# Cross-attention of a decoder layer: row maxima turned once per unit and placed by a transfer, values and totals one group later

## The reference, cut to what matters

```python
q = (x @ Wq).reshape(B, N, HEADS, hd).transpose(0, 2, 1, 3)
k = (context @ Wk).reshape(B, M, HEADS, hd).transpose(0, 2, 1, 3)
v = (context @ Wv).reshape(B, M, HEADS, hd).transpose(0, 2, 1, 3)
scores = jnp.einsum('bhid,bhjd->bhij', q, k) * scale
scores = jnp.where(context_mask[:, None, None, :], scores, max_neg)
attn = jax.nn.softmax(scores, axis=-1)
out = jnp.einsum('bhij,bhjd->bhid', attn, v)
out = out.transpose(0, 2, 1, 3).reshape(B, N, DIM)
return out @ Wo
```

## Time and profile before

| | |
|---|---|
| median of 3 runs | 3777.01 us (3770.28 to 3780.96) |
| profiled execution | 3775.88 us, span 3774.1 us, mean granted clock 0.982 |
| TensorE busy | 3639.7 us, 96% of the span, 28244 instructions |
| VectorE, ScalarE, GpSimd | 63%, 46%, 35% |
| hardware transfer queue | 318.26 MB, 30.7% of 16 DMA engines |

### The profile page before, as it was taken

How to read it: one execution, slowest core, us unless ns; L and a number is a source line. 1 busy time by engine, 2 the same in 40 slices (tenths; PEclk the granted TensorE clock), 3 DMA queues, 4 the chain that set the end, 5 groups by cost and what they waited for, 6 DMA issues and landing times. The chain is left out here.

```text
span 3774.1 us, 84215 instructions
## 1 busy us (share of the span) xinstructions
PE 3639.7 (96%) x28244; PEld 3139.7 (83%) x28244; DVE 2361.0 (63%) x5543; ACT 1731.9 (46%) x4278; POOL 1305.9 (35%) x1388
## 2 busy tenths in 40 slices
PE   8999999999979999999999999849999999999999
PEld 7888888888868888888888888638998899989998
DVE  6888888888846666666666666576433434434343
ACT  4555555555435555555555555413333333333332
POOL 2333333333325656666556566510101101011010
PEclk9999999999989999999999999869999999999999
DMA  4222222222243434444434343223324334234232
GB/s 127 60 54 63 54 63 53 64 53 64 72 122 94 112 106 104 108 116 107 121 96 113 104 108 97 71 68 94 121 82 122 107 98 123 82 118 123 85 108 69
DMA packets 315057, 349.72 MB, mean 93 GB/s; under 512 B 45308, under 2 KB 232036, under 8 KB 314884
## 3 DMA queue, kind: packets, MB, share of 16 engines
q1 hardware_dynamic: 305796, 318.26, 30.7%
q0 software_dynamic: 9088, 29.17, 2.4%
HBM read 183.23 MB, written 38.91 MB: 59 GB/s over the span
## 5 line engine op out<-in xcount | busy, mean ns | idle before, releaser
L1627 DVE TENSOR_REDUCE x_mx<-x_psS 112x1 f32<-112x752 f32 x512 | 479.7, 937 | 382.2 <-PE x_psS L1180 378.6
L2423 DVE TENSOR_TENSOR hid<-e_psU,act_g 128x280 f32<-128x280 f32 x256 | 115.1, 450 | 622.6 <-PE e_psU L34 585.8
L1462 ACT ACTIVATE x_pt<-x_psE 125x448 f32<-125x448 f32 x768 | 389.6, 542 | 227.6 <-PE x_psE L1192 217.7
L1051 POOL TENSOR_TENSOR part<-x_pt 125x448 f32<-125x448 f32 x255 | 292.4, 1147 | 506.0 <-ACT x_pt L1462 497.1
L2049 POOL DMA_INDIRECT out<-ex_y,sidx x40 | 39.8, 995 | 1020.4 <-DVE ex_y L2457 1010.2
L635 POOL TENSOR_TENSOR qks<-qks,cos 128x448 f32<-128x448 f32 x128 | 148.1, 1157 | 657.0 <-DMA qks<-qk 657.0
L1180 PE MATMUL x_psS<-k_st,q_st 97*112 97x376 f32 x1024 | 287.9, 362 | 24.1 <-DMA k_st<-mk 16.3
L32 PE MATMUL e_psG<-ex_hi,g_hi 128*128 128x280 f32 x1024 | 304.2, 297 | 6.7 <-ACT act_g L2208 4.5
L32 PE MATMUL pj<-xT_hi,win_hi 128*128 128x224 f32 x1024 | 302.2, 295 | 4.0 <-PEq L185 3.9
L2208 ACT ACTIVATE act_g<-e_psG 128x280 f32<-128x280 f32 x256 | 103.7, 405 | 426.4 <-PE e_psG L34 412.1
L1053 POOL TENSOR_TENSOR part<-part,x_pt 125x448 f32<-125x448 f32 x255 | 292.3, 1146 | 20.0
(11 more groups left out here) (305 smaller groups left out, 10890.3 us busy)
## 6 DMA issues: line engine op xcount, KB each, us to landing
k_st<-kT SPq DMA_DIRECT2D x768, 93.8 KB, 2.2
raw_g<-in_L_ffn_wg SPq DMA_DIRECT2D x128, 256.0 KB
raw_u<-in_L_ffn_wu SPq DMA_DIRECT2D x128, 256.0 KB
raw_d<-in_L_ffn_wd SPq DMA_DIRECT2D x128, 256.0 KB
qks<-qk SPq DMA_DIRECT2D x512, 56.0 KB, 2.0
q_st<-qT SPq DMA_DIRECT2D x384, 56.0 KB, 2.0
ctxt<-in_ctx SPq DMA_DIRECT2D x16, 1125.0 KB
xt<-in_x SPq DMA_DIRECT2D x16, 448.0 KB, 3.7
```

What stands on the lines that cost most here:

```text
L1051: pool.tensor_tensor(part[:], pt[j][:, 0, :], pt[j][:, 1, :], ALU.add).then_inc(parted, 1)
L1462: act.activation(pt[j][:, i, :], psE[(j + i) % 2][0:KR, 0:2 * T], ACT.Exp, scale=XD ** -0.5).then_inc(exp_done, 1)
L1627: dve.tensor_reduce(mx[:, j, h:h + 1], psS[0:HT, :, 0:376], AX.XY, ALU.max).then_inc(s_taken, 1)
L2423: dve.tensor_tensor(h[ring][:, halves[s]], psU[:, 0:CH], act_g[i][:, halves[s]], ALU.mult).then_inc(S["mul"], 1)
```

## The change

The maxima of two heads (four columns of `x_mx`) are split on VectorE while they still lie by query (`split_max`: high and low part, negated, eight columns of `m_parts`). TensorE turns the eight columns in one transposition to 8 rows by 112 columns. ScalarE copies them to `m_row` (`out_max`), and SyncE places them with a transfer in rows 97 and 98 of `q_st` (`place_max`). TensorE waits for that transfer (`m_placed`) where it waited for the unit's bank. M0 is turned right after the fourth quarter's first scores. `place_k` and `place_q` are cut in two halves of two heads, and the `place_max` calls stand between them; that of M1_0 stands behind `load_ctx`.

The values of group n - 2 move from the end of group n - 1 to the second gap of the first quarter of group n, and the totals of n - 2 follow them directly. For that `pt` and `ptsum` of head 0 have two buffers; those of the other heads have one. `qT` shrinks to two blocks.

Units are placed anew: V04 from the first quarter of group 0 to its end, V00 from the first quarter of group 3 to its end, Q0 and C20 from the third quarter of group 2 to the first gap of the fourth, O1 from the first quarter of group 2 to the third. ScalarE's and VectorE's lists follow.

```diff
-UNITS = ("K10 V04 M1_0 K11 Q2 V05 Q3 M0_0 X0 X1 "
+UNITS = ("K10 M1_0 K11 Q2 V05 Q3 M0_0 X0 X1 V04 "
          "K20 V10 M1_1 K21 V11 V12 V13 N0 M0_1 N1 O0 L "
-         "K30 M1_2 O1 K31 V14 V15 C00 C10 Q0 C20 M0_2 C01 Q1 C11 "
-         "K00 C21 V00 M1_3 K01 V01 V02 V03 M0_3").split()
+         "K30 M1_2 K31 V14 V15 C00 C10 O1 M0_2 Q0 C20 C01 Q1 C11 "
+         "K00 C21 M1_3 K01 V01 V02 V03 M0_3 V00").split()
 U_PRE = "X0 X1 C00 C10 C20 C01 C11 C21 Q0 Q1 K00 K01 V00 V01 V02 V03".split()
...
-            qT = [sb(c, f"qT{i}", [P, KD, T], F32R) for i in range(2)]
+            qT = [sb(c, f"qT{i}", [P, 2, T], F32R) for i in range(2)]
...
-            less = sb(c, "x_less", [P, 1])
-            pt = [op.pt[0], sb(c, "x_pt1", [KR, 3, 2 * T]), op.pt[2], op.pt[3]]
+            m_parts, m_row = sb(c, "m_parts", [HT, 2, 8], F32R), sb(c, "m_row", [8, HT], F32R)
+            pt_first = [op.pt[0], sb(c, "x_pt0_odd", [KR, 3, 2 * T])]
+            pt_other = [sb(c, "x_pt1", [KR, 3, 2 * T]), op.pt[2], op.pt[3]]
             part, yT, rz = op.part, op.yT, op.rz
-            ptsum = [sb(c, f"ptsum{i}", [KR, T]) for i in range(8)]
+            sum_first = [sb(c, f"ptsum0_{i}", [KR, T]) for i in range(2)]
+            sum_other = [sb(c, f"ptsum{i}", [KR, T]) for i in range(1, 4)]
...
+            def max_placed(t, i):
+                return 32 * t + 16 * i + 16
...
+            def pt(g, j):
+                return pt_other[j - 1] if j else pt_first[g % 2]
+            def ptsum(g, j):
+                return sum_other[j - 1] if j else sum_first[g % 2]
...
+                    def place_max(u, g, i):
+                        hold(sp, gate, pj_free[u.bank], u.after)
+                        head = 4 * g + 2 * i
+                        sp.dma_start(q_st[97:99, head:head + 2, :].bitcast(F32), m_row[:].bitcast(F32)).then_inc(m_placed, 16)
...
+                    def place_k(t, b, g, units, heads=range(4)):
+                        if 0 in heads:
...
+                        near, far = range(2), range(2, 4)
                         if not last:
                             load_ctx(b + 1)
-                        place_k(t + 1, b, 1, [unit_of(b, "K10"), unit_of(b, "K11")])
-                        place_q(b, 1, [unit_of(b, "Q2"), unit_of(b, "Q3")])
+                        if not first:
+                            place_max(unit_of(b, "M1_0"), 3, 1)
+                        k_units = [unit_of(b, "K10"), unit_of(b, "K11")]
+                        place_k(t + 1, b, 1, k_units, near)
+                        place_max(unit_of(b, "M0_0"), 0, 0)
+                        place_k(t + 1, b, 1, k_units, far)
+                        q_units = [unit_of(b, "Q2"), unit_of(b, "Q3")]
+                        place_q(b, 1, q_units, near)
+                        place_max(unit_of(b, "M1_1"), 0, 1)
+                        place_q(b, 1, q_units, far)
                         if not below(b, 2):
                             load_res(b - 1)
                             store_rows(b - 2)
-                        place_k(t + 2, b, 2, [unit_of(b, "K20"), unit_of(b, "K21")])
+                        k_units = [unit_of(b, "K20"), unit_of(b, "K21")]
+                        place_k(t + 2, b, 2, k_units, near)
+                        place_max(unit_of(b, "M0_1"), 1, 0)
+                        place_k(t + 2, b, 2, k_units, far)
+                        place_max(unit_of(b, "M1_2"), 1, 1)
                         if more:
                             load_x(b + 2, unit_of(b, "X1"))
-                        place_k(t + 3, b, 3, [unit_of(b, "K30"), unit_of(b, "K31")])
+                        k_units = [unit_of(b, "K30"), unit_of(b, "K31")]
+                        place_k(t + 3, b, 3, k_units, near)
+                        place_max(unit_of(b, "M0_2"), 2, 0)
+                        place_k(t + 3, b, 3, k_units, far)
                         if not first:
                             store(b - 1, unit_of(b, "O1"))
                         if not last:
-                            place_q(b + 1, 0, [unit_of(b, "Q0"), unit_of(b, "Q1")])
-                        if not last:
-                            place_k(t + 4, b + 1, 0, [unit_of(b, "K00"), unit_of(b, "K01")])
+                            q_units = [unit_of(b, "Q0"), unit_of(b, "Q1")]
+                            place_q(b + 1, 0, q_units, near)
+                            place_max(unit_of(b, "M1_3"), 2, 1)
+                            place_q(b + 1, 0, q_units, far)
+                            k_units = [unit_of(b, "K00"), unit_of(b, "K01")]
+                            place_k(t + 4, b + 1, 0, k_units, near)
+                            place_max(unit_of(b, "M0_3"), 3, 0)
+                            place_k(t + 4, b + 1, 0, k_units, far)
+                        else:
+                            place_max(unit_of(b, "M1_3"), 2, 1)
+                            place_max(unit_of(b, "M0_3"), 3, 0)
...
                         for j in heads:
-                            n, out = 4 * t + j, ptsum[4 * (g % 2) + j]
+                            n, out, p = 4 * t + j, ptsum(g, j), pt(g, j)
...
+                            elif j == 1 and not below(t, 1):
+                                hold(pool, gate, z_full, t)
...
-                        pe.wait_ge(s_taken, 8 * t + 4 * i + 4)
+                        pe.wait_ge(m_split, 4 * t + 2 * i + 2)
                         o = bank(u)
-                        for n in range(4):
-                            m = pe.transpose(o[:, n * HT:(n + 1) * HT], mx[:, 2 * i + n // 2, n % 2:n % 2 + 1].to_broadcast((HT, P)),
-                                             ident[0:HT, 0:HT])
-                        m.then_inc(pj_full, 1)
+                        pe.transpose(o[0:8, 0:HT], m_parts[:, i, :].bitcast(F32), ident[0:HT, 0:HT]).then_inc(pj_full, 1)
...
                             elif j == 3:
-                                turn_max(U(f"M0_{g}"), n, 0)
                                 if g == 0 and not last:
                                     turn_x(U("X0"), b + 1, 0)
                                 elif g == 1 and old:
                                     turn_rows(U("N1"), b - 2, 1)
                                 elif g == 2 and not last:
+                                    project_q(U("Q0"), 0, U("X0"))
+                                    turn_ctx(U("C20"), b + 1, 2, 0)
                                     turn_ctx(U("C01"), b + 1, 0, 1)
                         def second_gap(g, j):
                             n, prev, pprev = t + g, not (first and g == 0), not (first and g < 2)
                             if j == 0:
-                                if g == 0:
-                                    project_v(U("V04"), 0, 4)
-                                elif g == 1:
+                                if pprev:
+                                    values(n - 2, (g + 2) % 4)
+                                    totals(n - 2, g)
+                                if g == 1:
                                     project_v(U("V10"), 1, 0)
                                 elif g == 3 and not last:
                                     turn_ctx(U("C21"), b + 1, 2, 1)
-                                    project_v(U("V00"), 0, 0)
                                 if prev:
                                     turn_max(U(f"M1_{g}"), n - 1, 1)
-                                if g == 2 and not first:
-                                    project_out(U("O1"), b - 1, 1)
                             elif j == 1:
-                                if pprev:
-                                    totals(n - 2, g)
                                 if g == 0:
                                     project_q(U("Q2"), 2)
...
-                                elif g == 2 and not last:
-                                    project_q(U("Q0"), 0, U("X0"))
-                                    turn_ctx(U("C20"), b + 1, 2, 0)
+                                elif g == 2 and not first:
+                                    project_out(U("O1"), b - 1, 1)
...
-                                if g == 0 and not last:
-                                    turn_x(U("X1"), b + 1, 1)
+                                if g == 0:
+                                    if not last:
+                                        turn_x(U("X1"), b + 1, 1)
+                                    project_v(U("V04"), 0, 4)
...
+                                elif not last:
+                                    project_v(U("V00"), 0, 0)
...
                                 scores(n, g, j, 0)
+                                if j == 3:
+                                    turn_max(U(f"M0_{g}"), n, 0)
                                 if prev:
-                                    if j == 0:
-                                        done(U(f"M0_{gp}") if g else unit_of(b - 1, "M0_3"))
-                                    elif j == 2:
-                                        done(U(f"M1_{g}"))
```

(58 more changed lines are left out.)

98 lines of the change are left out of this document (46 added, 52 removed).

## The result

The changed kernel takes 3935.43 us (median; 3931.19 to 3937.8) against 3774.77 us for the kernel before on the same chip (3770.28 to 3783.06): a ratio of 1.0422, 95% interval 1.0407 to 1.0436. It is 160.7 us slower. The profiled execution has a span of 3935.9 us.

A forecast was written before the change was run, and what follows sets the result against it. TensorE's instruction order was taken to bound the kernel. A batch of 83.2 - 3.1 + 3.0 + 7.6 + 2.3 = 93.0 us, +9.8 in 14 batches, gives 3776 + 137 = 3913 us; range 3780 to 3950.

The forecast's parts named there:

- removed from TensorE: Maxima turned once instead of four times save 1.7 us, totals beside values 1.4: 3.1 us a batch.
- stand for M1_0's copy: First group, third quarter: TensorE waits 7.6 us for M1_0's maxima, in 14 of 16 batches.
- clock behind the stand: TensorE runs at half clock after the stand, losing 2.3 us each time, between 0 and 3.0.
- other new waits: Lost filler, Q1's bank, V00's going and bank changes bring 3.0 us of waits a batch.
- When TensorE needs the copy: Pieces ahead of the first group's third-quarter scores sum to +10.8 us from the group's start.
- its lower bound: One transposition of eight maxima columns takes at least a quarter of four's 0.32 us, 0.08; 0.11 taken.
- the forecast's later bound: M1_0's copy lands 14.4 us after the context's issue at +4.7, so at +19.1; +18.4 taken.
- held behind the context, by the nearest row: M1_0's copy waits behind the context load like a one-row mask copy that landed 6.9 us after issue.
- the first rival: Copy on free engines, not held behind the context: lands in 2.1 to 2.9 us, about 3787 us, chance 0.14.
- The rival without it: TensorE stands for M1_0's copy but its clock does not fall: 3881 us, chance 0.12.
- V00's going uncovers 1.0 and fills 0.4: Fourth group: moving V00 from behind C21 uncovers about 1.0 us of wait; at the group's end it fills 0.4.
- case for a copy that is not held: M1_0's copy lands in 2.1 to 2.9 us, costing 0.6 to 1.1 us a batch: about 3787 us, chance 0.14.

The follow-up runs named there:

- e5_max_first: Changed kernel with M1_0's copy of maxima issued on SyncE ahead of the next batch's context and mask load: 3898.07 us, ratio 1.032.
- e11_ctx_act: Changed kernel with the context load alone, still 125 rows, issued on ScalarE's queue at the start of each batch's first group: 3819.32 us, ratio 1.0118.
- e2_mask_late: Changed kernel with the mask's broadcast load issued behind M1_0's copy instead of ahead of it: 3926.74 us, ratio 1.0393.
- e4_act_queue: Changed kernel with the maxima's transfers issued on ScalarE's queue instead of SyncE's: 3859.54 us, ratio 1.0211.
- e6_four_turns: e5_max_first with four transpositions of each unit's maxima in place of one: 3905.41 us, 7 us more than its base.

## Why the prediction was right

The mechanism, its place and its sign are as forecast. By its own terms, per batch:

| term | forecast | found |
|---|---|---|
| removed from TensorE | -3.1 | -3.1 (maxima 8 x 0.26; totals about 1.0) |
| stand for M1_0's copy | +7.6 | +7.1 (92.0 / 13) |
| clock behind the stand | +2.3 | +2.2 |
| other new waits | +3.0 | +3.0 |
| clock fall at the fourth group's end | none | +0.9 |
| not named by any row (remainder) | none | +0.9 |
| sum | +9.8 | +11.0 |

That -3.1 agrees is in part luck: the forecast had 1.7 for the maxima and 1.4 for the totals, where 2.1 and 1.0 were found.

**When TensorE needs the copy.** Forecast +10.8, found +10.8. The sum of pieces held although its parts were off: values and totals together take 2.79 us instead of 3.0, the transposition 0.03 instead of 0.11 (below the 0.08 that the forecast called its lower bound), and the pieces ahead of the values 3.31 instead of 2.97.

**When it lands.** Forecast +18.4, found +19.0. That is the context's issue plus 13.7 where the forecast's later bound has plus 14.4. The expected issue of the context, +4.7, was 0.6 early; M1_0's own issue, +9.1, was 0.5 early. Over 13 batches the stand is 5.2 to 8.1 us; the two of 5.2 us follow the two largest clock falls in the group before (2.6 us), after which TensorE itself comes late.

**Who holds it.** The prediction called it held behind the context, by the nearest row, and left open whether by shared engines. The runs settle it: a split into 112 and 13 rows takes most of it away (11.9 us left of 92.0), and with another queue and the engines still shared the copy passes the load. The Trainium skill's rule on the number of engines, weighed in the prediction, was one half of the reason; that both stood in one queue was the other, and the prediction had not asked for it. (A copy on free engines, which it calls "the first rival", is the second of its list.)

**The clock.** The stand's second price came, 6 us at 0.50 to 0.55 from 1669.16 to 1675.2. That stretch takes 6.04 us, and the same pieces 3.41 in e5_max_first, which has no stand there, so 2.6 are lost in this batch. Over the 13 batches it is 1.5 to 2.9, on average 2.2. The rival without it fell.

**The new waits.** Over the 13 batches of the ruler, TensorE's listed waits other than for M1_0's copy are 50.6 us (16.2 qT, 11.8 x_mx, 8.7 x_xT, 5.6 x_pt, 3.6 cT, and at M0 and M1 units 2.6 for qT and 2.1 for m_parts), 3.9 each, against 12.2 us or 0.9 each in the kernel before. The net 3.0 is the forecast's 3.0, but not by its parts: Q1 waits 1.25 (1.5 forecast); the fourth group's are 0.42 for an exponential and 0.92 for a maximum, and they stand in its last quarter, not behind C21. There the step "V00's going uncovers 1.0 and fills 0.4" has the wrong sign: V00 back at its old place, on e5_max_first, costs 1.9 us a batch (26 us / 14).

**What was missed** are the two rows of the table without a forecast. From the starts of the pieces from that last maximum to the end of K00 (4.05 us at full clock), eight of 14 fourth groups have lost 1.2 to 2.7 us to a clock fall, 13.1 us together, so 0.9 each over the 14. It follows waits of 0.16, 0.42 and 0.92 us within 3 us, none of them large. The other 0.9 is only what is left of 11.0 after the named terms, and its cause stays open. Together the two are more than the 1.2 us a batch, or 17 us, that the sum lacks; a stand 0.5 us shorter than forecast takes part of them back. The other 7 of the 24 us by which the forecast came out low lie in the first batch and the tail, which it left as they were, within 3 us.

**Why it is still slower without the stand.** e11_ctx_act is 43 us above the kernel before, 3.0 a batch by the ruler. The removed 3.1 is outweighed: by its listed waits (56.6 us in 13 batches, 3.4 a batch more than before), a remaining 0.9 of stand, the clock fall (in 6 of 14 fourth groups, 8.3 us, 0.6 a batch) and an unnamed rest of 1.2. So the prediction's case for a copy that is not held, 3787 us, was 32 us too fast, for the same two reasons (0.6 and 1.2 us a batch) and for waits 0.4 us above the forecast 3.0.

## What to carry to other kernels

A small copy that the critical engine waits for should not stand in one DMA queue with a large load of few engines. Count from the large load's issue to the landing of a copy behind it (here 14 us) and look what the queue must deliver in that time. In this kernel all three places tried in the queue held something; the load's row count and its queue were what helped. Where an engine has a short wait anyway, work removed beside it may buy little, and may cost clock. Price a cover before you take it away, and read the next maximum, bank or copy that becomes late: in this kernel each edit of the order brought another wait or cost clock.

## What the runs showed of the hardware that was not expected

- A load of 1125 KB in 125 rows runs at a DMA share of 0.33 and 126 GB/s; the same in 112 and 13 rows at 1.05 and 302 GB/s. The broadcast mask load behind it costs SyncE 3.60 to 3.86 us of issue in the first case and 0.36 in the second, so an issue's price can be that of the transfer ahead of it. It is so directly behind that transfer: 3.7 us later the same issue took 0.69 us (e2_mask_late).
- A one- or eight-row copy behind that load in its queue is through 13.7 to 14.65 us after the load's issue. With the load in flight in another queue, a copy is through 5.1 us after its own issue, and 5.9 in e4_act_queue (issued 1715.25, TensorE released 1721.19); its first packet comes 4.0 to 5.9 us after the issue where a quiet one's comes after 1.4.
- TensorE's clock fell from 2.4 to 1.2 GHz also where no wait was longer than 0.92 us, in eight of 14 places of the same kind, and in 13 of 14 in e5_max_first. In e6_four_turns, which adds only transpositions (0.2 to 0.3 us at each of two places in the group), it stayed up in all 14; the wait there is 0.2 us shorter.
